# Softmax attention: both tiles' values ahead of the first transposes of probabilities, and the queries' low part right behind the normalised heads

## The chip, the cores and the metric

The kernel runs on one core of one Trainium2 chip. The metric is the device time of one execution in microseconds (us), as a median of several runs. All data are float32; some matrix products split their operands into a high part (rounded to the type fp32r) and a low part (the rest), and add three products of such parts.

## The reference, cut to what matters

The program is a stack of six layers on `x` (64 sequences of 64 tokens, 256 wide). The change touches only the fifth, a causal softmax self-attention with 16 heads of width 16:

```python
def _L1_attn_ref(x, Wqkv, Wout, bout):          # x is layer-normalised
    qkv = x @ Wqkv.T
    q, k, v = jnp.split(qkv, 3, axis=-1)        # then split in 16 heads
    dots = jnp.einsum('bhid,bhjd->bhij', q, k) * 16 ** -0.5
    dots = jnp.where(causal_mask, -jnp.inf, dots)
    attn = jax.nn.softmax(dots, axis=-1)
    out = jnp.einsum('bhij,bhjd->bhid', attn, v)
    return out.reshape(b, t, d) @ Wout.T + bout
x = x + _L1_attn_ref(_layernorm(x), ...)
```

## The kernel before, in words

The six layers run one after another; `x` stays on the chip in the tile `X` (`g_x` in the trace). The layer at hand is `softmax_attention` (lines 969 to 1375). A tile of `X` is 128 rows, two sequences; there are 32 tiles, worked on in 16 pairs (`NP` = 16). A software pipeline of steps runs over the pairs: in step `s`, pair `s` is normalised, pair `p = s-1` is projected to keys, queries and values, pair `a = s-2` gets scores and probabilities, and pair `e = s-3` gets attended values, the division by the sum, and the output projection. Four steps are written out, then a loop turns over two steps at a time, then the last steps are written out.

Each engine has its own program for a step; it works strictly in the order written, and engines wait for one another only through semaphores. So the order inside each engine's `step` is set by hand. For one step:

- **TensorE (PE)**: transposes of the normalised pair `p` into `ps_a` (line 1334; it waits for `xn_ready`, and for `q_ready` because the queries of the pair before still lie in `ps_a`), `attended(e, 0)` and `(e, 1)` (line 1289), `transposes(e, 3)` (line 1271), keys of group 0 (line 1312, into `ps_b`; waits for `xT_ready`), `attended(e, 2)`, keys of group 1, `attended(e, 3)`, `scores(a)` (line 1261, 96 products), queries (line 1312, into `ps_a`), `values(0)` (line 1319, into `ps_b`), `transposes(a, 0)`, `values(1)`, the transposes of the heads of `e` (line 1298), `transposes(a, 1)`, `projected_heads` (line 1306), `transposes(a, 2)`. `transposes(a, j)` takes the probabilities of a quarter `j` and waits for its exponential.
- **VectorE (DVE)**: low part of `xT` (line 1117), statistics, low part of the keys (line 1130), `maximum(a, 0)` and `(a, 1)` (mask added, line 1086, and row maxima, line 1090), `normalised_heads` (lines 1094, 1096), `maximum(a, 2)` and `(a, 3)`, normalised rows `xn` (line 1149), low part of the queries `q2[:, pp, 1]` (line 1154, which raises `q_ready`), `added(e, ...)` (line 1104).
- **ScalarE (ACT)**: high part of `xT` (line 1212), `transposed(e, 3)` (line 1173, copies transposed probabilities out of PSUM), high part of the keys (line 1184), `probabilities(a, 0)` (line 1168, the exponential), high part of the queries (line 1226, raises `q_high`), `probabilities(a, 1)`, `transposed(a, 0)`, `heads_out` twice (line 1179), `transposed(a, 1)`, `probabilities(a, 2)`, `values(p)` (lines 1195 and 1199), `transposed(a, 2)`, `probabilities(a, 3)`.
- **GpSimd (POOL)**: inverse standard deviation (lines 1061, 1064), four times scores minus row maximum (`shifted`, line 1071), the output bias added to `X` (line 1077).
- **SyncE (SP)**: four DMAs (line 1038) that move half of the values to other partitions. They wait for `vs_ready`, and what they bring is first read by `attended` two steps later.

In the trace the tiles of this layer are called `sa_...`, as are those of the third layer; lines 1061 to 1334 tell them apart.

Of the kernel before, what the change touches and what calls it, by code (L numbers as in the profile page):

```python
# [29 lines left out]
ALU = mybir.AluOpType  # L30
# [4 lines left out]
B, T, S, E = 64, 64, 256, 256  # L35
H, D = 16, 16
# [65 lines left out]
def live(t, n=NT):  # L102

    return not isinstance(t, int) or 0 <= t < n
# [864 lines left out]
def softmax_attention(nc, c, X, d):  # L969

    NP = NT // 2
    with ExitStack() as ctx:
# [13 lines left out]
        q2 = ph.sb("q2", [P, 2, 2, KC * 2, 2, P + T], F32R)  # L986
# [94 lines left out]
        @block.vector  # L1081
        def _(dve):
            def maximum(a, j):
                dve.wait_ge(s_done, 4 * a + j + 1)
                wait(dve, shift_ready, 4 * a + j - 1)
                nc.vector.tensor_tensor(masked[:, j % 2, :, :], ps_s[j][:, :].rearrange("p (n t) -> p n t", t=T),
                                        mask[:, :].unsqueeze(1).to_broadcast([P, 8, T]), ALU.add)\
                    .then_inc(masked_ready, 1)
                dve.wait_ge(masked_ready, 4 * a + j + 1)
                nc.vector.tensor_reduce(top[:, j % 2, :], masked[:, j % 2, :, :], AX.X, ALU.max).then_inc(top_ready, 1)  # L1090

            def normalised_heads(e, i):
                heads = ps_o[i][:, 0:H * D1].rearrange("p (h d) -> p h d", d=D1)
                nc.vector.reciprocal(rz[:, i, :], heads[:, :, D]).then_inc(rz_ready, 1)
                dve.wait_ge(rz_ready, 2 * e + i + 1)
                nc.vector.tensor_tensor(y[:, i, :, :], heads[:, :, 0:D],
                                        rz[:, i, :].unsqueeze(2).to_broadcast([P, H, D]), ALU.mult)\
                    .then_inc(y_ready, 1)

            def added(e, i):  # L1100
                dve.wait_ge(o_done, 2 * e + i + 1)
                if i == 0:
                    dve.wait_ge(bias_added, e + 1)
                nc.vector.tensor_tensor(X[:, 2 * e + i, :], X[:, 2 * e + i, :], ps_o[i][:, E:2 * E], ALU.add)\
                    .then_inc(x_updated, 1)

            dve.wait_ge(loaded, 16 * 5)
            dve.wait_ge(w_high, 1)
            nc.vector.tensor_tensor(wqkv2[:, 1, :, :], wqkv[:, :, :], wqkv2[:, 0, :, :], ALU.subtract)\
                .then_inc(w_split, 1)  # L1110

            def step(s, par):
                p, a, e = s - 1, s - 2, s - 3
                pp = 1 - par
                if live(p, NP):
                    dve.wait_ge(xT_high, p + 1)
                    nc.vector.tensor_tensor(xT[:, 1, :, :], ps_a[:, :].rearrange("p (k t) -> p k t", k=KC),
                                            xT[:, 0, :, :], ALU.subtract).then_inc(xT_ready, 1)
                if live(s, NP):
                    for i in range(2):  # L1120
                        nc.vector.bn_stats(stats[:, i, :], X[:, 2 * s + i, :]).then_inc(stats_done, 1)
                    for i in range(2):
                        wait_apart(dve, stats_done, 2 * s + i + 1, c.passed_dve)
                        ins = nc.vector.bn_aggr(mv[:, par, i, :], stats[:, i, :])
                    ins.then_inc(var_ready, 1)
                if live(p, NP):
                    dve.wait_ge(k_high, p + 1)
                    for g in range(KC):
                        for h2 in range(2):
                            ins = nc.vector.scalar_tensor_tensor(  # L1130
                                k2[:, pp, 1, g, :, h2, :], ps_b[:, g * 2 * P:(g + 1) * 2 * P]
                                .rearrange("p (i t) -> p i t", i=2), in_pair[:, h2:h2 + 1],
                                k2[:, pp, 0, g, :, h2, :], ALU.mult, ALU.subtract)
                    ins.then_inc(k_ready, 1)
                if live(a, NP):
                    maximum(a, 0)
                    maximum(a, 1)
                if live(e, NP):
                    dve.wait_ge(pv_done, 4 * e + 4)
                    for i in range(2):  # L1140
                        normalised_heads(e, i)
                if live(a, NP):
                    maximum(a, 2)
                    maximum(a, 3)
                if live(s, NP):
                    dve.wait_ge(rstd_ready, s + 1)
                    wait(dve, xT_done, s - 1)
                    for i in range(2):
                        ins = nc.vector.tensor_scalar(xn[:, par, i, :], X[:, 2 * s + i, :], mv[:, par, i, 0:1],
                                                      rstd[:, par, 1, i:i + 1], ALU.subtract, ALU.mult)  # L1150
                    ins.then_inc(xn_ready, 1)
                if live(p, NP):
                    dve.wait_ge(q_high, p + 1)
                    nc.vector.scalar_tensor_tensor(q2[:, pp, 1, :, :, 0:T].rearrange("p n b t -> p (n b) t"),
                                                   ps_a[:, :].rearrange("p (n t) -> p n t", t=T), D ** -0.5,
                                                   q2[:, pp, 0, :, :, 0:T].rearrange("p n b t -> p (n b) t"),
                                                   ALU.mult, ALU.subtract).then_inc(q_ready, 1)
                if live(e, NP):
                    for i in range(2):
                        added(e, i)  # L1160
            tile_steps(dve, step, n=NP, lag=3)

        @block.scalar
# [82 lines left out]
        def _(pe):  # L1246
# [70 lines left out]
            def values(i):  # L1317
                for n, (k, (x, z)) in enumerate((k, xz) for k in range(KC) for xz in THREE_PASSES):
                    mm = nc.tensor.matmul(ps_b[:, i * E:(i + 1) * E], xT[:, x, k, i * P:(i + 1) * P],
                                          wqkv2[:, z, k, 2 * E:3 * E], start=(n == 0), stop=(n == 3 * KC - 1))  # L1320
                return mm
# [4 lines left out]
            def step(s, par):  # L1326
                p, a, e = s - 1, s - 2, s - 3
                pp, ap, ep = 1 - par, par, 1 - par
                if live(p, NP):
                    pe.wait_ge(xn_ready, p + 1)  # L1330
                    wait(pe, q_ready, p)
                    for k in range(KC):
                        for i in range(2):
                            mm = nc.tensor.transpose(ps_a[:, (2 * k + i) * P:(2 * k + i + 1) * P],
                                                     xn[:, pp, i, k * P:(k + 1) * P], c.ident[:, :])
                    mm.then_inc(xT_done, 1)
                if live(e, NP):
                    attended(e, ep, 0)
                    attended(e, ep, 1)
                    transposes(e, 3)  # L1340
                if live(p, NP):
                    pe.wait_ge(xT_ready, p + 1)
                    wait(pe, v_ready, p)
                    keys_or_queries(ps_b, E, 0)
                if live(e, NP):
                    attended(e, ep, 2)
                if live(p, NP):
                    keys_or_queries(ps_b, E, 1).then_inc(k_done, 1)
                if live(e, NP):
                    attended(e, ep, 3)  # L1350
                if live(a, NP):
                    scores(a, ap)
                if live(p, NP):
                    keys_or_queries(ps_a, 0, 0)
                    keys_or_queries(ps_a, 0, 1).then_inc(q_done, 1)
                    pe.wait_ge(k_ready, p + 1)
                    values(0)
                if live(a, NP):
                    transposes(a, 0)
                if live(p, NP):  # L1360
                    values(1).then_inc(v_done, 1)
                if live(e, NP):
                    heads_transposed(e, 0)
                    heads_transposed(e, 1)
                if live(a, NP):
                    transposes(a, 1)
                if live(e, NP):
                    projected_heads(e, 0)
                    projected_heads(e, 1)
                if live(a, NP):  # L1370
                    transposes(a, 2)
# [1135 lines left out]
```

## Time and profile before

| | us |
|---|---|
| median of 3 runs | 2430.57 |
| lowest and highest of them | 2427.62, 2439.83 |
| the profiled execution, own time | 2439.46 |
| its span in the trace | 2437.7 |
| PE busy in the span | 2143.7 (88%) |
| DVE, ACT, POOL busy | 1493.9, 1098.7, 981.1 |
| this layer's steps in the span | about 1796 to 2082 |

The span is the part of the execution that the profiler's records cover. A row of the timeline gives the start and the duration in us, the engine and line, what is written from what, how many instructions were merged, and, in brackets, how long the engine stood idle before and what it waited for. PE's ends are modelled, so a following row may start slightly before the end of the one above.

### The profile page before, as it was taken

The numbers are of one execution on the slowest core, as the hardware profiler recorded it, in microseconds if no ns is written. First come the engines' busy times: TensorE is split into PE (matmuls) and PEld (weight loads), VectorE is DVE, ScalarE is ACT, GpSimd is POOL, SyncE is SP. The second block draws the span as 40 slices with busy tenths as digits, with TensorE's granted clock in tenths as the row PEclk, the third lists the DMA queues.
The fourth block names the chain that finished last, engine by engine and source line by source line (L and its number), as shares of the span: only waits on it lengthen the run. The fifth ranks groups of instructions, "written<-read, shape, count | busy, mean of one in ns | idle before, by whom it ended". The sixth has DMA issues, their size and how long they took to land. (4 is left out here: it accounts for less than half of the span.)

```text
span 2437.7 us, 57593 instructions
## 1 busy us (share of the span) xinstructions
PE 2143.7 (88%) x19514; PEld 1597.1 (66%) x19527; DVE 1493.9 (61%) x4179; ACT 1098.7 (45%) x2377; POOL 981.1 (40%) x1105
## 2 busy tenths in 40 slices
PE   4999999999879998998999999969968888477773
PEld 3888888888779986565666666646658877233332
DVE  3777777777556654882333333347757776587772
ACT  2666666666534442283222222223335554335442
POOL 3444445444300003343666666611133343035455
PEclk9999999999878978999999999989989999789996
DMA  4110111100011003041222222245510000000002
GB/s 131 32 30 29 29 29 30 38 29 29 8 20 11 9 10 106 0 190 33 85 85 84 87 86 86 82 167 205 191 25 8 9 8 8 35 1 1 0 0 69
DMA packets 120654, 128.80 MB, mean 53 GB/s; under 512 B 77681, under 2 KB 95218, under 8 KB 119282
## 3 DMA queue, kind: packets, MB, share of 16 engines
q1 hardware_dynamic: 106306, 89.77, 12.1%
q0 software_dynamic: 13824, 37.77, 5.0%
q8 instruction: 54, 0.88, 0.2%
q14 instruction: 38, 0.31, 0.0%
q10 hardware_dynamic: 432, 0.07, 0.0%
HBM read 96.11 MB, written 27.26 MB: 51 GB/s over the span
## 5 line engine op out<-in xcount | busy, mean ns | idle before, releaser
L426 ACT ACTIVATE xa_prob<-xa_neg_s,xa_neg_max 128x256 f32<-128x256 f32 x512 | 224.5, 499 | 142.5 <-DVE xa_neg_max L314 142.5
L1847 PE MATMUL ex_ps_h<-moew_w,ex_xT 128*128 x576 | 275.1, 600 | 4.1 <-issue 2.3
L314 DVE CUSTOM_DVE_ANT_0 xa_neg_s<-xa_ps_s,xa_mask 128x256 f32<-128x256 f32 x512 | 191.4, 421 | 37.6 <-PE xa_ps_s L480 22.0
L1895 DVE COPY ex_xT<-ex_ps_x 128x256 f32<-128x256 f32 x144 | 61.1, 425 | 247.9 <-PE ex_ps_x L1854 116.7
L1824 POOL DMA_INDIRECT ex_xg<-xn_rows,moe_in_row x144 | 139.6, 970 | 110.3 <-issue 63.2
L509 PEld LDWEIGHTS xa_ps_o<-xa_v,xa_probT 128*64 128x64 f32 x4096 | 141.3, 138 | 48.3 <-issue 43.0
L433 ACT ACTIVATE xa_probT<-xa_ps_s 128x512 f32<-128x512 f32 x256 | 152.0, 594 | 42.1 <-PE xa_ps_s L491 39.6
L509 PE MATMUL xa_ps_o<-xa_v,xa_probT 128*64 128x34 f32 x4096 | 170.2, 228 | 0.0
L1829 POOL DMA_INDIRECT expert_outs<-ex_y,moe_out_row x144 | 142.1, 987 | 62.0 <-issue 35.9
L491 PE MATMUL xa_ps_s<-g_ident,xa_prob 128*128 128x128 f32 x1024 | 164.1, 283 | 2.9 <-ACT xa_prob L426 2.4
L1880 ACT ACTIVATE ex_act_g<-ex_ps_h 128x256 f32<-128x256 f32 x144 | 55.2, 383 | 244.7 <-PE ex_ps_h L1847 144.7
L1861 PE MATMUL ex_ps_y<-moew_xw,ex_gT 128*128 x576 | 148.4, 380 | 1.2 <-DVE ex_gT L1905 1.2
L1847 PEld LDWEIGHTS ex_ps_h<-moew_w,ex_xT 128*128 128x128 f32 x576 | 98.6, 191 | 77.2 <-issue 76.3
L2335 PE MATMUL ff_ps_y<-ff_h,ff_tap 128*128 128x512 f32 x256 | 132.0, 641 | 7.9 <-DVE ff_y L2191 7.5
L2138 POOL TENSOR_TENSOR ff_y<-ff_y,ff_scale_b 128x512 f32<-128x512 f32 x64 | 82.0, 1282 | 103.1 <-ACT ff_scale_b L2269 103.1
L491 PEld LDWEIGHTS xa_ps_s<-g_ident,xa_prob 128*128 128x128 f32 x1024 | 112.7, 142 | 11.2 <-ACT xa_prob L426 4.0
L1973 PE MATMUL xb_ps_g<-xb_ctx_rows 128*128 128x256 f32 x512 | 118.8, 386 | 0.0
L1071 POOL TENSOR_TENSOR sa_shifted<-sa_masked,sa_top 128x512 f32<-128x512 f32 x64 | 68.1, 1064 | 123.1 <-DVE sa_top L1090 123.1
L270 POOL TENSOR_TENSOR xa_qz<-xa_q,xa_in_pair 128x256 fp32r<-128x256 f32 x128 | 74.5, 613 | 87.1 <-DVE xa_q L362 87.1
L1973 PEld LDWEIGHTS xb_ps_g<-xb_ctx_rows 128*128 128x128 f32 x512 | 96.7, 194 | 12.5
L1861 PEld LDWEIGHTS ex_ps_y<-moew_xw,ex_gT 128*128 128x128 f32 x576 | 98.3, 190 | 9.5 <-issue 2.1
L1884 ACT ACTIVATE ex_y<-ex_ps_y 128x256 f32<-128x256 f32 x144 | 55.2, 383 | 98.9 <-PE ex_ps_y L1861 78.0
(314 smaller groups left out, 5027.8 us busy)
## 6 DMA issues: line engine op xcount, KB each, us to landing
xa_ctxT<-in_ctxT_dram SPq DMA_DIRECT2D x32, 512.0 KB, 3.6
xb_ctx_rows<-in_ctx_rows_dram SPq DMA_DIRECT2D x32, 512.0 KB, 3.7
xb_expert_y<-expert_outs SPq DMA_DIRECT2D x32, 512.0 KB, 4.5
moew_w<-in_moe_w_dram SPq DMA_DIRECT2D x8, 1024.0 KB, 13.2
g_x<-in_x_dram SPq DMA_DIRECT2D x4, 1024.0 KB, 9.6
sa_v<-sa_vs SPq DMA_DIRECT2D x128, 32.0 KB, 2.2
xn_rows<-rs_xn SPq DMA_DIRECT2D x8, 512.0 KB, 2.9
moew_xw<-in_moe_w_dram SPq DMA_DIRECT2D x8, 512.0 KB, 20.7
```

What stands on the lines that cost most here:

```text
L314: ins = nc.vector.tensor_tensor_reduce(neg_s[:, u % 2, g, :], ps_s[j][:, g * S:(g + 1) * S], mask[:, b, :], -1.0, 3e38, ALU.add, ALU.min, ...
L426: ins = nc.scalar.activation(prob[:, u % 2, i, :], neg_s[:, u % 2, i, :], ACT.Exp, bias=neg_max[:, u % 2, i:i + 1], scale=-1.0)
L433: nc.scalar.activation(probT[:, u % 2, :, :, :].rearrange("p i c t -> p (i c t)"), ps_s[u % 4][:, :], ACT.Copy).then_inc(t_ready, 1)
L491: mm = nc.tensor.transpose(ps_s[u % 4][:, k:k + P], prob[:, u % 2, g, ch * P:(ch + 1) * P], c.ident[:, :])
L509: mm = nc.tensor.matmul(ps_o[b][rows, q * 2 * D1:(q + 1) * 2 * D1], probT[:, u % 2, g, ch, rows], v[:, ap, 2 * b + ch, 2 * q:2 * q + 2, :] ...
L1824: nc.gpsimd.indirect_dma_start(xg[:, s % 4, :], None, rows, bass.IndirectOffsetOnAxis(ap=c.in_row[:, s:s + 1], axis=0)).then_inc(x_loaded[ ...
L1829: nc.gpsimd.indirect_dma_start(c.y_dram[:, :], bass.IndirectOffsetOnAxis(ap=c.out_row[:, e:e + 1], axis=0), y[:, e % 4, :], None).then_inc ...
L1847: mm = nc.tensor.matmul(ps_h[1 - par][:, :], xT[:, 1 - par, k, :], c.w1[:, own, k, :], start=(k == 0), stop=(k == KC - 1))
L1861: mm = nc.tensor.matmul(ps_y[1 - par][:, 0:E], gT[:, 1 - par, k, :], c.w2[:, own, k, :], start=(k == 0), stop=(k == KC - 1))
L1973: mm = nc.tensor.matmul(ps_g[tp][b][:, g * E:(g + 1) * E], ctx_rows[:, tq, 2 * b + k, g * P:(g + 1) * P], ctx_rows[:, tq, 2 * b + k, :], s ...
L2138: nc.gpsimd.tensor_tensor(y[:, gp, j, :], y[:, gp, j, :], scale_b[:, gp, :], ALU.mult)\
L2335: mm = nc.tensor.matmul(ps_y[j % 2][:, :], tap[:, i, j, :], h[:, j % 4, :, 2 * i:2 * i + T], start=(i == 0), stop=(i == 1))
```

## The change: what it does

Two pieces of code move inside a step; nothing is added or taken away.

```diff
 # DVE
                     for i in range(2):
                         normalised_heads(e, i)
+                if live(p, NP):
+                    dve.wait_ge(q_high, p + 1)
+                    nc.vector.scalar_tensor_tensor(q2[:, pp, 1, ...], ps_a[...], D ** -0.5,
+                                                   q2[:, pp, 0, ...], ALU.mult, ALU.subtract).then_inc(q_ready, 1)
                 if live(a, NP):
                     maximum(a, 2)
                     maximum(a, 3)
...
                     ins.then_inc(xn_ready, 1)
-                if live(p, NP):
-                    dve.wait_ge(q_high, p + 1)
-                    nc.vector.scalar_tensor_tensor(q2[:, pp, 1, ...], ps_a[...], D ** -0.5,
-                                                   q2[:, pp, 0, ...], ALU.mult, ALU.subtract).then_inc(q_ready, 1)
                 if live(e, NP):
                     for i in range(2):
                         added(e, i)
 # PE
                     pe.wait_ge(k_ready, p + 1)
                     values(0)
+                    values(1).then_inc(v_done, 1)
                 if live(a, NP):
                     transposes(a, 0)
-                if live(p, NP):
-                    values(1).then_inc(v_done, 1)
                 if live(e, NP):
                     heads_transposed(e, 0)
                     heads_transposed(e, 1)
```

On PE, in the loop of this layer from the scores on, the order before is (`sa_ps_b<-sa_wqkv,sa_xT` are the values, `sa_ps_s<-g_ident,sa_prob` the transposes of probabilities):

```order
L1261 MATMUL sa_ps_s<-sa_k,sa_q 128x128 x96
L1312 MATMUL sa_ps_a<-sa_xT,sa_wqkv 128x256 x12
L1319 MATMUL sa_ps_b<-sa_wqkv,sa_xT 128x256 x6
L1269 REGISTER_ALU
L1271 MATMUL sa_ps_s<-g_ident,sa_prob 128x128 x4
L1319 MATMUL sa_ps_b<-sa_wqkv,sa_xT 128x256 x6
L1296 REGISTER_ALU
L1298 MATMUL sa_ps_o<-g_ident,sa_y 128x128 x2
```

and with the change:

```order
L1261 MATMUL sa_ps_s<-sa_k,sa_q 128x128 x96
L1312 MATMUL sa_ps_a<-sa_xT,sa_wqkv 128x256 x12
L1319 MATMUL sa_ps_b<-sa_wqkv,sa_xT 128x256 x12
L1269 REGISTER_ALU
L1271 MATMUL sa_ps_s<-g_ident,sa_prob 128x128 x4
L1296 REGISTER_ALU
L1298 MATMUL sa_ps_o<-g_ident,sa_y 128x128 x2
```

The second six products of the values have gone ahead of the first transposes; the rest of PE's order is as it was.

On DVE, in the same loop from the second head normalisation on (`sa_q<-sa_ps_a,sa_q` is the queries' low part, `sa_masked` and `sa_top` are `maximum`), before:

```order
L1096 TENSOR_TENSOR sa_y<-sa_ps_o,sa_rz 128x256
L1084 REGISTER_ALU
L1086 TENSOR_TENSOR sa_masked<-sa_ps_s,sa_mask 128x512
L1090 TENSOR_REDUCE sa_top<-sa_masked 128x8
L1084 REGISTER_ALU
L1086 TENSOR_TENSOR sa_masked<-sa_ps_s,sa_mask 128x512
L1090 TENSOR_REDUCE sa_top<-sa_masked 128x8
L1146 REGISTER_ALU
L1149 TENSOR_SCALAR sa_xn<-g_x,sa_ln_mv,sa_ln_rstd 128x256 x2
L1154 SCALAR_TENSOR_TENSOR sa_q<-sa_ps_a,sa_q 128x8x64
L1104 ISA
L1104 TENSOR_TENSOR g_x<-g_x,sa_ps_o 128x256
```

and with the change:

```order
L1096 TENSOR_TENSOR sa_y<-sa_ps_o,sa_rz 128x256
L1144 SCALAR_TENSOR_TENSOR sa_q<-sa_ps_a,sa_q 128x8x64
L1084 REGISTER_ALU
L1086 TENSOR_TENSOR sa_masked<-sa_ps_s,sa_mask 128x512
L1090 TENSOR_REDUCE sa_top<-sa_masked 128x8
L1084 REGISTER_ALU
L1086 TENSOR_TENSOR sa_masked<-sa_ps_s,sa_mask 128x512
L1090 TENSOR_REDUCE sa_top<-sa_masked 128x8
L1152 REGISTER_ALU
L1155 TENSOR_SCALAR sa_xn<-g_x,sa_ln_mv,sa_ln_rstd 128x256 x2
L1104 ISA
L1104 TENSOR_TENSOR g_x<-g_x,sa_ps_o 128x256
```

One instruction has moved from behind `xn` to ahead of two maxima. The orders of ACT, POOL and SP are the same in both kernels.

## Rows read from the trace of the kernel before

**Rows 1.** Busy time of each engine in one step; the columns stand first.
```profile
core 0: us, PE busy (x) PEld busy (x) DVE busy (x) ACT busy (x) POOL busy (x), PEclk, DMA share, GB/s
1930.80:1947.60 16.80, 14.93 (x234) 13.39 (x232) 12.31 (x26) 9.06 (x20) 6.61 (x8) 1.00 0.08 8
```
**Rows 2.** Timeline of PE, the scores of pairs 0, 3 and 12.
```profile
1814.02 2.90 PE L1261 MATMUL sa_ps_s<-sa_k,sa_q 32*128 32x128 f32 x96
...
1863.67 2.90 PE L1261 MATMUL sa_ps_s<-sa_k,sa_q 32*128 32x128 f32 x96
...
2014.58 2.90 PE L1261 MATMUL sa_ps_s<-sa_k,sa_q 32*128 32x128 f32 x96
```
**Rows 3.** Timeline of PE, one step from scores to the next keys.
```profile
1930.75 2.90 PE L1261 MATMUL sa_ps_s<-sa_k,sa_q 32*128 32x128 f32 x96
1933.58 1.67 PE L1312 MATMUL sa_ps_a<-sa_xT,sa_wqkv 128*128 128x256 f32 x12
1935.09 0.87 PE L1319 MATMUL sa_ps_b<-sa_wqkv,sa_xT 128*128 128x256 f32 x6
1937.19 0.66 PE L1271 MATMUL sa_ps_s<-g_ident,sa_prob 128*128 128x128 f32 x4 [1.22 <-ACT sa_prob L1168]
...
1941.17 0.60 PE L1271 MATMUL sa_ps_s<-g_ident,sa_prob 128*128 128x128 f32 x4
1942.41 0.66 PE L1334 MATMUL sa_ps_a<-g_ident,sa_xn 128*128 128x128 f32 x4 [0.64 <-DVE sa_q L1154]
1943.07 1.13 PE L1289 MATMUL sa_ps_o<-sa_v,sa_w 128*64 128x34 f32 x32
...
1944.54 0.95 PE L1312 MATMUL sa_ps_b<-sa_xT,sa_wqkv 128*128 128x256 f32 x6
```
**Rows 4.** Timeline of DVE in the same step.
```profile
1933.77 0.69 DVE L1086 TENSOR_TENSOR sa_masked<-sa_ps_s,sa_mask 128x512 f32<-128x512 f32 x1 [0.24 <-PE sa_ps_s L1261]
...
1937.33 0.42 DVE L1096 TENSOR_TENSOR sa_y<-sa_ps_o,sa_rz 128x256 f32<-128x256 f32 x1
1937.67 0.68 DVE L1086 TENSOR_TENSOR sa_masked<-sa_ps_s,sa_mask 128x512 f32<-128x512 f32 x1
...
1940.30 1.45 DVE L1149 TENSOR_SCALAR sa_xn<-g_x,sa_ln_mv,sa_ln_rstd 128x256 f32 x2
1941.68 0.68 DVE L1154 SCALAR_TENSOR_TENSOR sa_q<-sa_ps_a,sa_q 128x512 fp32r<-128x512 f32 x1
1942.28 0.73 DVE L1104 TENSOR_TENSOR g_x<-g_x,sa_ps_o 128x256 f32 x2
1943.73 0.69 DVE L1117 TENSOR_TENSOR sa_xT<-sa_ps_a,sa_xT 128x512 fp32r<-128x512 f32 x1 [0.72 <-ACT sa_xT L1212]
```
**Rows 5.** Timeline of ACT in the same step.
```profile
1937.04 0.58 ACT L1226 ACTIVATE sa_q<-sa_ps_a 128x512 fp32r<-128x512 f32 x1
...
1940.22 0.63 ACT L1168 ACTIVATE sa_prob<-sa_shifted 128x512 f32<-128x512 f32 x1
1940.76 0.58 ACT L1195 ACTIVATE sa_vs<-sa_ps_b 128x512 f32<-128x512 f32 x1
1941.24 0.77 ACT L1199 ACTIVATE sa_v<-sa_ps_b 64x256 f32<-64x256 f32 x2
1942.03 0.60 ACT L1173 ACTIVATE sa_w<-sa_ps_s 128x512 f32<-128x512 f32 x1
1942.53 0.62 ACT L1168 ACTIVATE sa_prob<-sa_shifted 128x512 f32<-128x512 f32 x1
1943.11 0.60 ACT L1212 ACTIVATE sa_xT<-sa_ps_a 128x512 fp32r<-128x512 f32 x1
```
**Rows 6.** Timeline of POOL in the same step.
```profile
1939.15 1.04 POOL L1071 TENSOR_TENSOR sa_shifted<-sa_masked,sa_top 128x512 f32<-128x512 f32 x1 [1.52 <-DVE sa_top L1090]
1940.47 1.14 POOL L1071 TENSOR_TENSOR sa_shifted<-sa_masked,sa_top 128x512 f32<-128x512 f32 x1 [0.28 <-DVE sa_top L1090]
```
**Rows 7.** Timeline of ACT, the third exponential in the last step with projections.
```profile
2057.58 0.63 ACT L1168 ACTIVATE sa_prob<-sa_shifted 128x512 f32<-128x512 f32 x1 [0.31 <-POOL sa_shifted L1071]
```

More of the change, by code:

```diff
@@ L1141, in step @@
                         normalised_heads(e, i)
+                if live(p, NP):
+                    dve.wait_ge(q_high, p + 1)
+                    nc.vector.scalar_tensor_tensor(q2[:, pp, 1, :, :, 0:T].rearrange("p n b t -> p (n b) t"),
+                                                   ps_a[:, :].rearrange("p (n t) -> p n t", t=T), D ** -0.5,
+                                                   q2[:, pp, 0, :, :, 0:T].rearrange("p n b t -> p (n b) t"),
+                                                   ALU.mult, ALU.subtract).then_inc(q_ready, 1)
                 if live(a, NP):
@@ L1151, in step @@
                     ins.then_inc(xn_ready, 1)
-                if live(p, NP):
-                    dve.wait_ge(q_high, p + 1)
[L1154 to L1157, printed above, removed]
                 if live(e, NP):
```

## The prediction

> **What bounds the kernel now.** The change stays inside the softmax attention, whose steps lie between 1796 and 2082 us of a span of 2437.7 us; the other layers' instructions are the same. So I read this stage alone: first the busy time of one step, then the starts of the scores, which give the period, then each engine's timeline through one step. In a step of 16.8 us PE is busy for 14.93 us at a granted clock of 1.00, DVE 12.31, ACT 9.06 and POOL 6.61 [rows 1]. No engine is full, so the period is set by a loop of waits that runs across engines. From pair 3 to pair 12 nine periods take 2014.58 - 1863.67 = 150.91 us, 16.77 us each [rows 2].
>
> PE is idle at two places of a step: 1.22 us before the first transposes of probabilities, where it waits for the exponential, and 0.64 us before the transposes of `xn`, where the trace names DVE's low part of the queries [rows 3]. The change aims at both. What has to be asked is whether they lie on the loop. I follow it back from the scores. They come behind the keys with a fixed stretch of PE work. The keys start at 1944.54 [rows 3], just behind DVE's low part of `xT`, which ends at 1943.73 + 0.69 = 1944.42 [rows 4]; that waited 0.72 us for ACT's high part (1943.11 to 1943.71) [rows 5]; that waited for PE's transposes of `xn` (1942.41 to 1943.07) [rows 3]; those for DVE. DVE starts the first masking 0.24 us after it fell idle, released by the scores, and from there to `added` at 1942.28 it shows no idle time at all [rows 4]. So the loop is: scores, some 8.6 us of DVE without a gap (1933.77 to 1942.36), transposes of `xn`, high part, low part, keys, scores. The 1.22 us before the first transposes of probabilities are not in it.
>
> A second path is nearly as long, and it is the one to watch. ACT's third exponential starts at 1940.22, right when POOL's third `shifted` ends (1939.15 + 1.04 = 1940.19) [rows 5, 6]. Behind it ACT has the values, a copy and the fourth exponential, all back to back, and only then the high part of `xT` at 1943.11 [rows 5]. The fourth exponential ends, by its row, at 1943.15, later than PE's transposes of `xn` at 1943.07: both let the high part go within 0.1 us of each other [rows 3, 5].
>
> **Part 1, values(1) ahead of transposes(a, 0).** Six products of 0.87 us as a group go into the gap of 1.22 us. The twelve queries start at 1933.58 and the six values behind them at 1935.09, so twelve need 1.51 us of PE, and all twelve values are issued by 1935.09 + 1.51 = 1936.60 and modelled to end by 1936.76. The exponential they must not delay ends about 0.05 us before 1937.19 [rows 3], so 0.4 us of the gap is left and the transposes lose nothing. Everything behind them on PE could come up to 0.8 us earlier. But the second transposes wait for their own exponential, the head projections for ACT's `heads_out`, and the third transposes (1941.17 now) for the third exponential, which ends at 1940.85; the transposes of `xn` behind them wait for DVE until 1942.41 anyway [rows 3, 5]. So PE gives the gained time back as a longer wait there. Value of part 1: 0. If the cover were gone, that is if DVE were not late at 1942.41, it would be worth up to the 0.87 us a step.
>
> **Part 2, the queries' low part ahead of maximum(a, 2).** It costs DVE 1942.28 - 1941.68 = 0.60 us from start to start [rows 4]. In the new place it needs the high part of the queries, which ends at 1937.04 + 0.58 = 1937.62 [rows 5], and DVE is free for it at 1937.67 [rows 4]: it starts with no wait. `q_ready` then comes at about 1938.35 instead of 1942.36. But PE's transposes of `xn` need `xn_ready` as well, and `xn` now runs 0.60 us later: 1940.90 to 1942.35, where the old order had `q_ready` at 1942.36. DVE does the same work between the scores and this release, so the release doesn't move; only the name of what PE waits for changes, from the queries' low part to `xn`. `added` starts at 1942.28 as before. Gain: 0, within the 0.1 us that two kinds of release may differ by.
>
> What is late is what stands behind it on DVE. Both later maxima come 0.60 us later, so POOL's third `shifted` runs from 1939.75 to 1940.79, and the third exponential starts at 1940.82 instead of 1940.22. ACT's queue behind it has no slack: 2.31 us from the third exponential to the fourth, and about 0.54 us from an exponential to what follows it (1940.22 to 1940.76), 2.85 us together [rows 5]. The high part of `xT` can start at 1940.82 + 2.85 = 1943.67 instead of 1943.11, though PE has its input ready at 1943.07: 0.56 us late. DVE's low part follows 0.62 us behind (1943.73 - 1943.11), at 1944.29, and ends at 1944.98. The keys need some 0.06 us more (in the other turn of the loop I take the two to follow closely, so I allow no more), so 1945.04 instead of 1944.54: **0.50 us late**. From there to the next scores PE has only its own work, so the whole loop is 0.50 us longer: 17.27 us a step instead of 16.77. The loop through ACT's queue has become the longest, and the loop through DVE and `xn` has half a microsecond of slack.
>
> How often: the delay passes from a step with maxima and projections to a next step with projections. Maxima run in steps 2 to 17, projections in steps 1 to 16, so there are 14 such passages (2 to 3, up to 15 to 16). The first are slightly different, since no heads are there yet, but the third exponential is there too. In step 16 there is no `xn` any more, yet the queries' low part still stands ahead of the third maximum; ACT waits for POOL there already by 0.31 us [rows 7], so the fourth exponential and the last scores' release shift by the full 0.60. Sum: 14 x 0.50 + 0.60 = **7.6 us longer**.
>
> The bounds of one passage: the low end is 0, if ACT's queue packs closer than now or the releases hide it (below 0 only if the DVE loop got shorter, and its work is the same); the high end is 0.68 us, the duration of the moved instruction [rows 4], so 0 to 16 x 0.68 = 10.9 us. I take 0.50, since each link of the chain has its row.
>
> The values are written out by ACT 0.6 us later too, and so are SP's four DMAs behind them. They are read two steps later, so this costs nothing.
>
> **Against the profile.** The sum goes on the profiled execution's 2439.46 us and would give 2447.1. That execution is 8.9 us above the median of the runs, 2430.57, near their highest, 2439.83. The stage gives no reason for that, so I add the difference to the median: 2430.57 + 7.6 = 2438.2 us. The 0.5% that a measurement of this kernel can tell from no change is 12.2 us.
>
> **The rivals.**
> *Hidden, no difference.* ACT catches up, for example because its copies overlap more when all their inputs are ready. Against it: ACT's rows from the third exponential on are packed already [rows 5]. It would give 2430.6 us.
>
> *Faster.* PE is 14.93 of 16.8 us busy [rows 1], the values fill 0.87 us of its idle time, and the named wait of 0.64 us for the queries' low part goes away. If PE's own queue set the period, the two places gave 0.87 + 0.64 = 1.51 us in 15 steps, 22.7 us: 2407.9. With only the first, 15 x 0.87 = 13 us: 2417.5. Against it: DVE is full from the masking to `added`, in whichever order its work stands [rows 4]. The Trainium skill leads one to this rival (Perfetto Trace Analysis, Optimization Strategies): keep the matmul engine as highly used as possible, and when it idles, speed up what blocks it. By that rule the named wait and the filled gap would count in full; the rows of DVE speak against it here. What speaks for this rival is a release that fires sooner from `xn` than from the queries' low part, or transposes that end sooner than modelled.
>
> *Clearly slower.* The place is the moved instruction itself, now at the head of DVE's queue with a wait of its own, for ACT's high part of the queries. That ends at 1937.62 and DVE comes to it at 1937.67, 0.05 us later [rows 4, 5]. In its old place the same wait had over 4 us to spare. If ACT's part, or its signal, comes later than the rows tell, DVE stands still in front of the two maxima, `xn` and `added`, and every tenth of a us goes on both loops in full. The nearest price of such a signal is the 0.24 us that DVE waits for the scores' release [rows 4]. The rival decides from 0.3 us of wait on: a passage then costs 0.80 us and all 15 some 12.2 us, the 0.5%. With 0.4 us, for a signal slower than any in these rows, it is 14 x 0.90 + 1.00 = 13.6 us: 2444.2. Against it: DVE starts the low part of `xT` 0.02 us after ACT's high part of it ends (1943.71 to 1943.73), the same kind of release [rows 4, 5].
>
> That the change doesn't do what it says can be left out: the order rows of both engines show it.
>
> **How the numbers follow.** Forecast 0.68; hidden, 0.14; faster, 0.06; clearly slower, 0.06; the rest, 0.06, for a passage that costs more than its bound. The predicted time is the forecast's, 2438.2. Its own range is 5 to 10.9 us of cost with some 3 us of scatter of a median of this kernel (the lowest run is 3 us below it): 2433 to 2445. With the hidden case and the scatter below it the range begins at 2429; with the clearly slower case it ends at 2446. Faster by over 0.5%: 0.05. Slower by over 0.5%, above 2442.7: the slower rival, the rest, and a small part of the forecast by scatter, 0.17. Within: 0.78.
>
> **What would show it.** Right: the scores 17.2 to 17.35 us apart; values in one group of twelve and PE's idle time before the first transposes down to some 0.4 us; PE waiting for `xn` at 1334, still about 11.65 us behind the scores; a new idle stretch of about 0.5 us before the keys, released by DVE's low part of `xT`; ACT waiting for POOL about 0.6 us or more before the third exponential and not at all for PE before the high part of `xT`. Wrong: a period at or under 16.77 us, or an idle stretch before the keys that is absent; for the slower rival an idle stretch of 0.3 us or more ahead of the moved instruction.

## The result, and the profile after

The changed kernel has a median of 2441.94 us (2439.82 to 2444.69, 5 runs), the kernel before 2429.56 us (2427.30 to 2439.83, 5 runs). The medians lie 12.4 us apart. The ratio taken over all runs is 1.0042, some 10 us, with a 95% interval from 1.0025 to 1.0059 (6 to 14 us): slower, but the runs don't settle on which side of the 0.5% named ahead. The median is 3.7 us above the forecast of 2438.2. The profiled executions (2439.82 us, span 2438.0; before 2439.46, span 2437.7) hardly differ, since the one of before lies at the top of its runs. Its extra time lies ahead of this stage: the scores of pair 0 start at 1814.02 us there, and at 1797.10 us in a second profile of the same program (`before_again` below). So the stage has to be compared by its own rows and not by the spans.

Timeline of PE in the changed kernel, the scores of pairs 0, 1, 3 and 12, and of a step in the middle up to the next scores, against [rows 2, 3] of before:

```profile
1804.30 5.39 PE L1261 MATMUL sa_ps_s<-sa_k,sa_q 32*128 32x128 f32 x96
1823.78 2.90 PE L1261 MATMUL sa_ps_s<-sa_k,sa_q 32*128 32x128 f32 x96
...
1858.20 2.90 PE L1261 MATMUL sa_ps_s<-sa_k,sa_q 32*128 32x128 f32 x96
...
1927.21 2.90 PE L1261 MATMUL sa_ps_s<-sa_k,sa_q 32*128 32x128 f32 x96
1930.04 1.67 PE L1312 MATMUL sa_ps_a<-sa_xT,sa_wqkv 128*128 128x256 f32 x12
1931.55 1.59 PE L1319 MATMUL sa_ps_b<-sa_wqkv,sa_xT 128*128 128x256 f32 x12
1933.65 0.66 PE L1271 MATMUL sa_ps_s<-g_ident,sa_prob 128*128 128x128 f32 x4 [0.50 <-ACT sa_prob L1168]
...
1937.96 0.66 PE L1271 MATMUL sa_ps_s<-g_ident,sa_prob 128*128 128x128 f32 x4 [0.41 <-ACT sa_prob L1168]
1938.95 0.65 PE L1334 MATMUL sa_ps_a<-g_ident,sa_xn 128*128 128x128 f32 x4 [0.33 <-DVE sa_xn L1155]
...
1941.47 0.99 PE L1312 MATMUL sa_ps_b<-sa_xT,sa_wqkv 128*128 128x256 f32 x6 [0.22 <-DVE sa_xT L1117]
...
2013.47 2.90 PE L1261 MATMUL sa_ps_s<-sa_k,sa_q 32*128 32x128 f32 x96
```

From pair 3 to pair 12 the scores are (2013.47 - 1858.20) / 9 = 17.25 us apart, 0.48 us more than the 16.77 of before. The values are one group of twelve, and PE's idle time ahead of the first transposes fell from 1.22 to 0.50 us. In its place PE waits 0.41 us ahead of the third transposes, 0.33 us (before 0.64) ahead of those of `xn`, now for `xn` by name, and for DVE's low part of `xT` ahead of the keys, which is new. That last wait is 0.22 us where the forecast had named about 0.5, although the keys are as late as forecast: in before the modelled end of the row ahead of them (1944.13 + 0.66 = 1944.79) lay behind their start (1944.54). The keys are 14.26 us behind the scores instead of 13.79.

Timelines of DVE and of ACT in the same step, against [rows 4, 5]:

```profile
1933.78 0.42 DVE L1096 TENSOR_TENSOR sa_y<-sa_ps_o,sa_rz 128x256 f32<-128x256 f32 x1
1934.12 0.68 DVE L1144 SCALAR_TENSOR_TENSOR sa_q<-sa_ps_a,sa_q 128x512 fp32r<-128x512 f32 x1
1934.72 0.68 DVE L1086 TENSOR_TENSOR sa_masked<-sa_ps_s,sa_mask 128x512 f32<-128x512 f32 x1
...
1940.72 0.69 DVE L1117 TENSOR_TENSOR sa_xT<-sa_ps_a,sa_xT 128x512 fp32r<-128x512 f32 x1 [1.25 <-ACT sa_xT L1212]
```

```profile
1937.28 0.63 ACT L1168 ACTIVATE sa_prob<-sa_shifted 128x512 f32<-128x512 f32 x1 [1.02 <-POOL sa_shifted L1071]
1937.82 0.58 ACT L1195 ACTIVATE sa_vs<-sa_ps_b 128x512 f32<-128x512 f32 x1
1938.29 0.77 ACT L1199 ACTIVATE sa_v<-sa_ps_b 64x256 f32<-64x256 f32 x2
1939.09 0.60 ACT L1173 ACTIVATE sa_w<-sa_ps_s 128x512 f32<-128x512 f32 x1
1939.58 0.62 ACT L1168 ACTIVATE sa_prob<-sa_shifted 128x512 f32<-128x512 f32 x1
1940.10 0.59 ACT L1212 ACTIVATE sa_xT<-sa_ps_a 128x512 fp32r<-128x512 f32 x1
```

DVE starts the moved instruction with no wait and the next masking 0.60 us later. ACT stands idle for 1.02 us until the third exponential, then works without a gap to the high part of `xT`, 2.82 us later, though PE's transposes of `xn` were done 0.50 us before that. DVE's wait for the high part grew from 0.72 to 1.25 us.

The rest is at the ends. From the scores of pair 1 to those of pair 15 the changed kernel needs 2062.88 - 1823.78 = 239.10 us, before 2062.49 - 1830.22 = 232.27: 6.8 us more. The one passage from pair 0 to pair 1 took 19.48 us instead of 16.20, 3.3 us more, where the forecast had 0.5. The two make 10.1 us, which agrees with the ratio (10.2 us) and lies inside its interval; the medians are 2 us further apart. Behind the last scores the two kernels run the same order.

### The profile page after: what moved, and what is told of

The parts are those of the page before. It is cut to its first block and busy times, and to the rows that moved or that the text cites. A ratio compares the mean times of both kernels' runs of the same rounds, so it can differ in the third digit from the quotient of the medians.

```text
span 2438.0 us, 57593 instructions
## 1 busy us (share of the span) xinstructions
PE 2150.4 (88%) x19514; PEld 1592.0 (65%) x19527; DVE 1491.0 (61%) x4179; ACT 1094.6 (45%) x2377; POOL 980.9 (40%) x1105
```

## The experiments

All were compared with the kernel before on the chip that they ran on. The period is the mean distance of the scores from the third pair on, the passage that from pair 0 to pair 1.

| run | ratio to before (95%) | period, us | passage, us |
|---|---|---|---|
| before, two profiles | | 16.77, 16.77 | 16.20, 16.20 |
| the whole change | 1.0042 (1.0025 to 1.0059) | 17.25 | 19.48 |
| after_again | 1.0047 (1.0030 to 1.0065) | 17.25 | 19.62 |
| pe_only | 1.0017 (1.0008 to 1.0027) | 16.77 | 18.61 |
| dve_only | 1.0048 (1.0035 to 1.0061) | 17.25 | 19.16 |
| low_before_xn | 1.0004 (0.9994 to 1.0014) | 16.65 | 18.31 |
| act_values_first | 1.0084 (1.0071 to 1.0097) | 17.18 | 23.60 |
| copy_later | 1.0026 (1.0014 to 1.0038) | 16.90 | 19.14 |
| pe_only_step2_old | 1.0000 (0.9987 to 1.0013) | 16.77 | 16.19 |
| step2_old | 1.0028 (1.0018 to 1.0038) | 17.25 | 16.21 |
| banks_act | 0.9967 (0.9954 to 0.9980) | 16.18 | 15.64 |
| banks_xn | 0.9983 (0.9972 to 0.9994) | 16.27 | 15.88 |

**Which half of the change costs?** First each half alone.

> Only TensorE's part of the change: all twelve value products ahead of the first transposes of probabilities; VectorE's order as before. My theory (the period is set by VectorE between scores and xn, the gap on TensorE is off the loop): period 16.77 us as before, TensorE's idle time before the first transposes falls from 1.22 to 0.4-0.5 us and comes back ahead of the transposes of xn; time within 2 us of before. Rival 'TensorE's gap counts': 0.87 us less per step, period 15.9 us, 13 us faster. Rival 'the cost of the whole change sits here': about 10 us slower.

> Only VectorE's part: the queries' low part behind the normalised heads; TensorE's order as before. Theory (ScalarE's queue behind the third exponential carries the 0.60 us to the high part of xT): period 17.25 us, as in the whole change, the keys waiting for VectorE's low part of xT; 7 to 8 us slower by the steps alone. Rival 'the two parts need each other to be slow' or 'the cost is TensorE's': period 16.77, no difference.

The period answers at once: TensorE's half leaves it at 16.77 us, VectorE's half alone makes it 17.25. In the first, PE's wait for `q_ready` grew to 0.85 us: the last of the filled gap came back there. The rest had been given back on the way, for the third transposes start only 0.24 us earlier than in before (10.18 against 10.42 us behind the scores). The ratio of `pe_only` was a miss, though: 4 us slower where I had allowed 2. Its passage of 18.61 us, 2.4 over before, is where that lies.

**Does the cost hang on the place, and does it go through ScalarE's queue?** Three kernels keep the whole change but for one thing each (`act_values_first` moves it on two engines).

> The whole change, but the queries' low part stands between the fourth maximum and xn instead of behind the heads. The third exponential is then not delayed. Theory: ScalarE's queue is back at its old time, so the 0.5 us a step are gone: period 16.7 us (VectorE's part of the loop even some 0.3 us shorter, since the low part now fills time in which xn was held behind GpSimd's fourth subtraction, but ScalarE's queue has only 0.05 to 0.1 us to give), time 0 to 2 us below before. Rival 'an earlier low part of any kind costs' (its wait for ScalarE's high part, its reading of PSUM beside TensorE's writes): period stays at 17.2.

```diff
-    # low part of the queries behind normalised_heads
     maximum(a, 2); maximum(a, 3)
+    # low part of the queries here
     # xn
```

Period 16.65 us (expected 16.7), no measurable difference in the total. So an earlier low part costs nothing by itself; what costs is that two maxima stand behind it. Timeline of DVE in this kernel, in a step whose scores start at 1915.40, and of ACT:

```profile
1924.94 0.68 DVE L1147 SCALAR_TENSOR_TENSOR sa_q<-sa_ps_a,sa_q 128x512 fp32r<-128x512 f32 x1
1925.54 1.08 DVE L1155 TENSOR_SCALAR sa_xn<-g_x,sa_ln_mv,sa_ln_rstd 128x256 f32 x2
```

```profile
1924.86 0.63 ACT L1168 ACTIVATE sa_prob<-sa_shifted 128x512 f32<-128x512 f32 x1 [0.41 <-POOL sa_shifted L1071]
...
1927.69 0.59 ACT L1212 ACTIVATE sa_xT<-sa_ps_a 128x512 fp32r<-128x512 f32 x1
```

The high part starts 12.29 us behind the scores, before 12.36, in the changed kernel 12.89. The pair of `xn` takes 1.08 us instead of the 1.45 of [rows 4]. In before its second instruction alone took 1.13 us and ended 0.14 us behind POOL's fourth `shifted` [rows 6]; with the low part between, less of that time is spent waiting. The Trainium skill (SBUF — State Buffer, Who interferes with whom) says that a VectorE instruction in a two-port mode and a GpSimd one shut each other out until the first has ended; the 0.37 us agree with it. DVE frees `xn` 0.3 us earlier by that, but ACT's queue lets through only 0.1.

> The whole change with VectorE's order kept as changed, but TensorE computes the values before the queries, and ScalarE writes them out ahead of the first exponential, where it stood idle 4.67 us, and not behind the third. That takes 1.27 us out of ScalarE's queue between the third exponential and the high part of xT. Theory: the delayed third exponential no longer reaches the keys in full; what is left is the third transposes, the copy and the fourth exponential: high part of xT at most 0.1 us later than in before, period 16.77 to 16.9 us, time 0 to 2 us above before. Rival 'the cost lies on VectorE itself' (the moved instruction lengthens the loop): period stays at 17.25, 7 us or more slower.

```diff
 # PE: values ahead of the queries; ACT:
     high_keys(pp, 1)
+    values(p, pp)
     probabilities(a, 0)
...
     probabilities(a, 2)
-    values(p, pp)
     transposed(a, 2)
```

A miss on the period, 17.18 us instead of at most 16.9. Timelines of ACT and DVE in this kernel, scores at 1933.16:

```profile
1938.29 0.78 ACT L1199 ACTIVATE sa_v<-sa_ps_b 64x256 f32<-64x256 f32 x2
1939.10 0.63 ACT L1168 ACTIVATE sa_prob<-sa_shifted 128x512 f32<-128x512 f32 x1
1939.75 0.60 ACT L1227 ACTIVATE sa_q<-sa_ps_a 128x512 fp32r<-128x512 f32 x1
...
1943.54 0.63 ACT L1168 ACTIVATE sa_prob<-sa_shifted 128x512 f32<-128x512 f32 x1 [1.16 <-POOL sa_shifted L1071]
1944.92 0.60 ACT L1173 ACTIVATE sa_w<-sa_ps_s 128x512 f32<-128x512 f32 x1 [0.75 <-PE sa_ps_s L1270]
```

```profile
1940.38 0.69 DVE L1144 SCALAR_TENSOR_TENSOR sa_q<-sa_ps_a,sa_q 128x512 fp32r<-128x512 f32 x1 [0.23 <-ACT sa_q L1227]
```

The queue from the third exponential to the high part did shrink, from 2.82 to 2.39 us (1943.54 to 1945.93). But the values, written out just ahead of the first exponential, push that and the high part of the queries back, and DVE now waits 0.23 us for it at the head of its queue, ahead of the maxima. That is the mechanism of my slower rival, put there by my own edit. The kernel loses more at the start: in step 1 the queries stand behind values that wait 3.35 us for the low keys, and the scores of pair 0 come 20.48 us behind the first transposes of `xn` instead of 15.76.

A cleaner test of the queue is this one, which moves one copy and nothing else:

> The whole change, but ScalarE makes the third copy of transposed probabilities behind the high part of xT instead of ahead of the fourth exponential. Nothing else moves; TensorE reads that copy only after the keys of group 0. This takes one link of 0.49 us out of ScalarE's queue between the delayed third exponential and the high part of xT. Theory (that queue carries the delay of 0.60 us): the high part starts 12.4 us behind the scores instead of 12.9, as in before (12.36), and the period is 16.77 to 16.85 us; what is left over before is the fill, 2 to 4 us. Rival (the loop is longer by the moved instruction itself, on VectorE): period stays at 17.25 us and the time at 10 us over before.

```diff
 # ACT, step s
     # high part of xT
+    transposed(e, 2)
     transposed(e, 3)
...
-    transposed(a, 2)
     probabilities(a, 3)
```

Period 16.90 us, close above the expected 16.85: of the 0.48 us that the change had added, 0.35 are gone. Timeline of ACT, scores at 1920.28:

```profile
1932.16 0.63 ACT L1168 ACTIVATE sa_prob<-sa_shifted 128x512 f32<-128x512 f32 x1
1932.82 0.60 ACT L1212 ACTIVATE sa_xT<-sa_ps_a 128x512 fp32r<-128x512 f32 x1
```

The high part starts 12.54 us behind the scores, down from 12.89, the same 0.35. What is left over before (0.13 us) is in that queue too: the high part still starts right at the end of the fourth exponential (1932.16 + 0.63 = 1932.79). VectorE's order is that of the change, so the loop is not longer by the moved instruction itself. It goes through ScalarE's queue.

**Where do the other 2 to 3 us come from?** Each kernel above had a longer first passage than before.

> The kernel before itself, a second profile. In its first profile the passage from the scores of pair 0 to those of pair 1 took 16.20 us with TensorE at full clock throughout; in all five changed kernels so far it took 18.3 to 23.6 us, with TensorE's transposes and keys there at half clock. Theory A (the order of the changed kernels makes TensorE idle more in that step, so the clock falls there): 16.2 us again here. Theory B (the fall comes or goes by chance, whatever the order): some 18 to 19 us here as well.

> TensorE's part of the change alone, but step 2, the first with scores, keeps the old order. TensorE's part alone measured 1.0017 of before with an unchanged period of 16.76 us, and its profile had 2.4 us more in the passage from pair 0 to pair 1, at half clock. Theory A (the order of step 2 makes the clock fall): the passage is 16.2 us again, and the time is that of before within 1 us. Theory B (chance): a passage of 18 us or more is as likely here, and the ratio stays at 1.001 to 1.002.

Against `pe_only`:

```diff
                     values(0)
-                    values(1).then_inc(v_done, 1)
+                    if not (isinstance(s, int) and s == 2):
+                        values(1).then_inc(v_done, 1)
                 if live(a, NP):
                     transposes(a, 0)
+                if live(p, NP) and isinstance(s, int) and s == 2:
+                    values(1).then_inc(v_done, 1)
```

> The changed kernel itself once more, beside before on the same chip, to have it next to the run below. The steps alone account for 14 x 0.485 + 0.6 = 7.4 us. Its first profile had 19.48 us in the passage from pair 0 to pair 1 instead of 16.20, with TensorE at half clock. Theory A (the order of step 2 makes the clock fall): again 18.5 us or more in that passage, and 10 to 11 us slower in all, ratio 1.004 to 1.0045. Theory B (chance): any value from 16.7 us, and 7 to 8 us slower.

> The whole change except in step 2, which keeps the old order on both engines. Theory A: passage from pair 0 to pair 1 at 16.2 us with TensorE at full clock, period behind it 17.25 us, so 13 x 0.485 + 0.6 = 6.9 us slower than before, ratio 1.0025 to 1.0035, some 3 us under the run of the whole change. Theory B: no difference from the whole change beyond 0.5 us.

The edit of `step2_old` does the same on PE, and on DVE it keeps the queries' low part behind `xn` in step 2.

Busy time and granted clock of core 0 in stretches of the passage; the columns are stretch and length, busy time of PE, PEld, DVE, ACT and POOL, PE's clock, DMA share, GB/s. In `before_again`, scores of pair 0 at 1797.10:

```profile
1797.10:1803.10 6.00, 5.22 (x115) 4.94 (x114) 4.22 (x9) 1.73 (x5) 1.34 (x2) 1.00 0.03 2
1803.10:1807.10 4.00, 2.27 (x17) 1.89 (x18) 3.93 (x8) 3.53 (x7) 3.23 (x3) 1.00 0.01 2
1807.10:1810.10 3.00, 2.60 (x44) 1.98 (x42) 1.15 (x3) 2.41 (x6) 1.41 (x2) 1.00 0.26 31
1810.10:1813.10 3.00, 2.82 (x43) 2.48 (x42) 1.04 (x5) 0.88 (x2) 0.93 (x2) 1.00 0.21 18
```

In `after_again`, scores of pair 0 at 1806.40:

```profile
1806.40:1812.40 6.00, 5.96 (x121) 5.68 (x120) 4.22 (x8) 1.72 (x5) 1.36 (x2) 1.00 0.03 3
1812.40:1816.40 4.00, 1.32 (x8) 0.84 (x8) 2.94 (x6) 2.67 (x5) 1.96 (x2) 1.00 0.00 2
1816.40:1819.40 3.00, 1.91 (x12) 1.34 (x14) 1.69 (x3) 2.81 (x7) 2.49 (x4) 0.75 0.12 16
1819.40:1822.40 3.00, 3.00 (x39) 2.93 (x37) 1.57 (x5) 0.76 (x3) 0.85 (x3) 0.50 0.34 33
```

In `pe_only`, scores of pair 0 at 1799.76:

```profile
1805.76:1809.76 4.00, 1.61 (x11) 1.14 (x12) 3.93 (x8) 3.55 (x7) 3.23 (x3) 1.00 0.01 2
1809.76:1812.76 3.00, 2.59 (x32) 2.06 (x30) 1.10 (x3) 2.45 (x6) 1.42 (x2) 0.58 0.26 32
```

And in `step2_old`, scores of pair 0 at 1797.82:

```profile
1803.82:1807.82 4.00, 2.27 (x17) 1.88 (x18) 3.93 (x8) 3.53 (x7) 3.23 (x3) 1.00 0.01 2
1807.82:1810.82 3.00, 2.60 (x44) 1.98 (x42) 1.15 (x3) 2.40 (x6) 1.43 (x2) 1.00 0.26 31
```

Two things are lost in this passage. The first is a wait on DVE. Timelines of DVE, ACT and PE in `after_again`:

```profile
1813.39 0.69 DVE L1144 SCALAR_TENSOR_TENSOR sa_q<-sa_ps_a,sa_q 128x512 fp32r<-128x512 f32 x1 [0.99 <-ACT sa_q L1226]
```

```profile
1816.56 0.63 ACT L1168 ACTIVATE sa_prob<-sa_shifted 128x512 f32<-128x512 f32 x1 [1.02 <-POOL sa_shifted L1071]
```

```profile
1817.24 0.66 PE L1271 MATMUL sa_ps_s<-g_ident,sa_prob 128*128 128x128 f32 x4 [2.34 <-ACT sa_prob L1168]
1818.15 1.12 PE L1334 MATMUL sa_ps_a<-g_ident,sa_xn 128*128 128x128 f32 x4 [0.25 <-DVE sa_xn L1155]
```

In a steady step the heads stand between the second maximum and the moved instruction (1936.42 to 1937.67 in before), and that work covers ACT's high part of the queries. In step 2 there are no heads, and DVE stands still for 0.99 us in front of the moved instruction (0.98 in the first profile of the change, 0.99 in `dve_only` and `copy_later`). The two maxima behind it come 1.7 us later than in before. The third exponential comes 1.1 us later, since ACT itself was late for it in before, and so does the high part of `xT`: 12.98 us behind the scores instead of 11.85.

The second is the clock. The values in one group fill the six us behind the scores (5.96 us busy instead of 5.22) and leave less PE work for the four us after them: 1.61 us instead of 2.27 in `pe_only`, and 1.32 where DVE's wait holds back the third exponential as well. Then the clock falls from 2.4 to 1.2 GHz. In step 2 there are no heads of an older pair that would fill that stretch; in all later steps up to the last scores there are, and the clock stays at 1.00. In `pe_only` the transposes of `xn` still start 10.76 us behind the scores (before_again 10.77), so all its 2.4 us are lost behind them, in PE work at the low clock. In `after_again` 3.4 - 1.1 = 2.3 us are.

With the old order in step 2 alone, on PE (`pe_only_step2_old`) or on both engines (`step2_old`), the clock does not fall, the passage is 16.2 us again, and the ratios drop from 1.0017 to 1.0000 and from 1.0047 to 1.0028. In each of these pairs the intervals overlap a little, but the passages don't: 16.2 us in all four profiles whose step 2 has both old orders, 18.3 us or more in all seven that have a new one on one or both. So I take theory A. In `dve_only` PE's order is the old one, and it is the late third exponential that leaves PE idle there, for 2.34 us. The kernel before has a low clock behind a wait as well, behind the scores of the last pair (granted clock 0.50 from 2068.60 to 2072.60):

```profile
2068.67 1.12 PE L1271 MATMUL sa_ps_s<-g_ident,sa_prob 128*128 128x128 f32 x4 [3.28 <-ACT sa_prob L1168]
```

What exactly decides isn't settled. The two runs with swapped banks, whose step 2 is different again, kept the short passage and the clock of 1.00 with 1.86 and 1.85 us of PE work in those four us, while in `dve_only` it fell with 1.97; and the longest single wait of PE in the passage is shorter in `pe_only`, where it fell (1.21 us), than in before (1.29 us). The first profile of the changed kernel lost its 3.3 us in part in another way. Its clock was low already at the scores of pair 0 (5.39 us for them), so that the first masking came 5.41 us behind the start of the scores instead of 3.29, 2.1 us late; it was back at 1.00 by the third transposes and did not fall again, and the other 1.2 us are the late third exponential. Why it was low there stays open, and `after_again`, the same program, was at 1.00 at that place.

The Trainium skill (Perfetto Trace Analysis, Matmul Optimizations) advises back-to-back matmuls in batches because the engine scales its power by use; here a batch made fuller left a hole behind it, and the hole counted.

**The aim by another way.** What bound the kernel before was DVE's work between scores and `xn`, in which the queries' low part stood because `ps_a` was wanted back. If the next transposes go to the other bank, that instruction can leave the loop.

> Not the change but its aim by another way. The two PSUM banks a and b swap roles from pair to pair, so that the next transposes of xn go where the values were and no longer wait for the queries' low part; that low part moves behind added, into the 0.72 us in which VectorE waited for ScalarE. Values come ahead of the queries on TensorE, ScalarE writes them out ahead of the first exponential, and the third copy of transposed probabilities goes behind the high part of xT. Theory: 0.60 us leave VectorE's part of the loop and ScalarE's queue is 1.3 us shorter behind the third exponential, so the period is 16.1 to 16.3 us and the time 7 to 9 us below before. Rival 'TensorE's own queue is the next bound at once': period 16.6 or more, under 3 us faster.

```diff
+                ps_a, ps_b = banks[pp], banks[1 - pp]      # on DVE, ACT and PE
 # PE
-                    wait(pe, q_ready, p)     # ahead of the transposes of xn
+                    wait(pe, v_ready, p)
...
-                    wait(pe, v_ready, p)     # ahead of the keys
+                    wait(pe, q_ready, p)
 # DVE: low part of the queries behind added(e, 0), added(e, 1)
```

On ACT the values also go ahead of the first exponential and the third copy behind the high part of `xT`, and on PE the values go ahead of the queries. It holds: period 16.18 us, ratio 0.9967, 8 us below before and, across chips, some 18 to 19 below the changed kernel. DVE's idle time ahead of the low part of `xT` fell to 0.20 us, the moved instruction lying in the rest. The run moves four things at once, so it shows that the aim can be reached and not what the banks alone are worth. The next step went too far (it also has the third copy back in its old place):

> As the run with swapped banks, but xn also stands ahead of the fourth maximum, and ScalarE takes the fourth exponential behind the high part of xT. xn then ends some 1.4 us earlier beside VectorE's loop. Theory: the loop no longer runs through VectorE; it runs through the third exponential, the third transposes and those of xn on TensorE: period 15.7 to 16.1 us, time 9 to 14 us below before. Rival 'the late fourth exponential holds TensorE's transposes ahead of the keys': period 16.2 or more, no better than with the banks alone.

Period 16.27 us, ratio 0.9983: no better than with the banks alone, as the rival had it. Timeline of PE and ACT in this kernel:

```profile
1924.53 1.13 PE L1293 MATMUL sa_ps_o<-sa_v,sa_w 128*64 128x34 f32 x32 [0.24 <-DVE g_x L1104]
1925.73 0.66 PE L1275 MATMUL sa_ps_s<-g_ident,sa_prob 128*128 128x128 f32 x4
```

```profile
1925.05 0.63 ACT L1170 ACTIVATE sa_prob<-sa_shifted 128x512 f32<-128x512 f32 x1
```

The fourth exponential ends at 1925.68 and PE's transposes of it start at 1925.73, in front of the keys. The attended values ahead of them end, as modelled, at 1925.66, so this path is as long: `xn` is early now, but they wait 0.24 us for `added`, which starts 10.92 us behind the scores (10.93 in `banks_act`), since DVE has the same work ahead of it. No run tells the two apart.

## Why the prediction was right, and where it was off

- **What bounds the kernel.** Right. The loop through DVE and the near second path through ACT's queue give the periods of before, the change, its two halves and `low_before_xn`, and `copy_later` to 0.05 us. The period of `act_values_first` was explained only behind its result.
- **Part 1, worth 0.** Right in the steady steps, 16.77 us. Its step "Value of part 1: 0" failed for step 2, which I had set equal to the others ("the first are slightly different"). There it takes work out of a stretch of PE, the clock falls, and 2.4 us are lost.
- **Part 2, 0.60 us on DVE with no wait, 0.50 us a passage.** In the steady steps the 0.60 is measured as such. In step 2 "it starts with no wait" was wrong: the margin of 0.05 us came from a step with heads, and without them DVE waits 0.99 us. A steady passage cost 0.48 us: high part of `xT` 0.53 us later (0.56 forecast), keys 0.47 later (0.50). The last passage, pair 14 to 15, went from 14.29 to 14.90 us, 0.61 (0.60).
- **The sum.** Without the first passage 13 x 0.50 + 0.60 = 7.1 us forecast, 6.8 measured. With that passage's 3.3 us in place of its 0.5 it is 10.1 us instead of 7.6. The term mis-sized is one passage of fourteen, by 2.8 us: 0.50 us forecast, 3.3 measured, of which some 1.1 to 1.2 us are the late third exponential, with DVE's wait, and some 2.1 to 2.3 the low clock. It made the result lie nearer to the 0.5% than I had it. Added to the 2430.57 us that the forecast started from it gives 2440.7; the other 1.2 us up to 2441.94 lie within the scatter of a median.
- **The rivals.** Hidden: no, ACT doesn't catch up. Faster: no; the named wait went from the queries' low part to `xn` and the loop was not shorter. Slower by a wait in front of the moved instruction: not in the steady steps of the change (0.0 us idle), but in its step 2 with 0.99 us, and in the step shown of `act_values_first` with 0.23 us. The low clock, which made up some 2 of the 10 us, was not among them.
- **Small misses.** `pe_only` by 2 us and `act_values_first` by 18 us in time and 0.3 us in period, for the first passage, the start and the late high part of the queries; `copy_later` by 0.05 us.

## What to carry to other kernels

When a trace names a wait, add up what its releaser's engine does from the loop's last event to the release: if it is full, reordering it moves the name of the wait and nothing else. Then look at who is served later by the new order, and whether another engine's queue behind that has slack; here it had 0.1 us against 0.6. A wait that earlier work covers in the steady step is bare where that work is missing. Treat the steps that fill a pipeline apart from the steady ones, since an order that closes a gap there can open a longer one and take the clock with it.

## What the runs showed of the hardware that I had not expected

The granted clock reacted to one step: in before, with PE busy 2.27 of 4 us, it stayed at 1.00; in the changed kernel (`after_again`), with 1.32 of 4 us, it was 0.50 within the next 6 us, and a group of four transposes took 1.12 us instead of 0.66. The busy time of that stretch does not tell the cases apart by itself: 1.86 us kept the clock in `banks_act`, 1.97 us did not in `dve_only`. And an instruction of DVE between the start of POOL's subtraction and `xn` is partly free: it cost 0.60 us by its start-to-start time, but in `low_before_xn` it shortened the pair behind it from 1.45 to 1.08 us.
